# Attention values turned round: v as weights, the turned probabilities streamed, and a row's sums inverted once and spread by matmul

## What is computed

```python
x = x + _L0_conv_ref(_gn(x), ...)     # attention
x = x + _L1_conv_ref(_gn(x), ...)     # 3 x 3 convolution

# attention: 7 x 7 windows (N = 49 tokens), 8 heads of 16 channels
q = q * hd ** (-0.5)
attn = jnp.einsum('whnd,whmd->whnm', q, k)
attn = attn + jnp.transpose(rpb, (2, 0, 1))[None]      # and the mask of the shift
attn = jax.nn.softmax(attn, axis=-1)
x = jnp.einsum('whnm,whmd->whnd', attn, v).transpose(0, 2, 1, 3).reshape(B * nW, N, C)
x = x @ proj_weight.T + proj_bias
```

## Time and profile before

| | before |
|---|---|
| median of 3 runs (lowest to highest) | 3633.04 us (3629.91 to 3636.04) |
| profiled run: time, span | 3628.35 us, 3626.5 us |
| PE busy, PEld busy | 3415.0 us (94%), 2799.3 us (77%) |
| DVE, ACT, POOL busy | 3045.9 (84%), 2630.5 (73%), 2322.2 (64%) |
| matmul passes on PE | 57227 |
| values, transposes of the probabilities, scores: passes | 16384, 4096, 16384 |
| mean granted TensorE clock | 0.995 |

### The profile page before, as it was taken

How to read it: one execution, slowest core, us unless ns; L and a number is a source line. 1 busy time by engine, 2 the same in 40 slices (tenths; PEclk the granted TensorE clock), 3 DMA queues, 4 the chain that set the end, 5 groups by cost and what they waited for, 6 DMA issues and landing times.

```text
span 3626.5 us, 141183 instructions
## 1 busy us (share of the span) xinstructions
PE 3415.0 (94%) x57227; PEld 2799.3 (77%) x57227; DVE 3045.9 (84%) x7552; ACT 2630.5 (73%) x5857; POOL 2322.2 (64%) x3674
## 2 busy tenths in 40 slices
PE   2999999999999999999999999999999999999997
PEld 1778778778778778778777778777778778788785
DVE  5788888888888888888888888888888888888885
ACT  1777777777777777777777777777777777777772
POOL 4476666766666766666766666766667766657763
PEclk9999999999999999999999999999999999999998
DMA  2011101111101111101111111111111111111001
GB/s 57 20 30 33 33 25 30 36 33 36 33 25 30 36 33 36 33 23 33 35 34 35 28 28 33 33 35 36 28 28 33 33 36 33 30 25 33 18 18 29
DMA packets 213331, 113.75 MB, mean 31 GB/s; under 512 B 8784, under 2 KB 212688, under 8 KB 212688
## 3 DMA queue, kind: packets, MB, share of 16 engines
q1 hardware_dynamic: 212688, 104.72, 11.0%
HBM read 53.31 MB, written 51.38 MB: 29 GB/s over the span
## 4 chain that ended last, share of the span: by engine, by line
PE 51%; DVE 23%; POOL 12%; issue 11%; ACT 2%; SPq 0%; DVEq 0%; POOLq 0%; DMA 0%; ACTq 0%
PE conv_ps L994 14%; PE qkv_ps L875 10%; PE attn_ps L913 7%; PE probsT_ps L899 7%; PE scores_ps L888 5%; DVE s_sb L743 4%; POOL s_sb L404 3%; DVE plane_lo L755 3%; PE misc_ps L875 2%; DVE s_max L748 2%; DVE x_b L791 2%; PE misc_ps L961 2%; PE misc_ps L957 2%; PE misc_ps L951 2%; POOL x_n L444 1%
## 5 line engine op out<-in xcount | busy, mean ns | idle before, releaser
L404 POOL TENSOR_TENSOR s_sb<-s_sb,s_max 113x392 f32<-113x392 f32 x1024 | 1027.7, 1004 | 1127.6 <-DVE s_max L748 1123.2
L899 PE MATMUL probsT_ps<-ident,probs 113*128 113x113 f32 x4096 | 586.4, 265 | 72.6 <-ACT probsT L466 72.5
L460 ACT ACTIVATE probs<-s_sb 113x392 f32<-113x392 f32 x1024 | 551.6, 539 | 128.3 <-POOL s_sb L404 124.8
L432 POOL TENSOR_TENSOR plane<-x_n 128x224 f32<-128x224 f32 x896 | 601.3, 692 | 18.7
L913 PEld LDWEIGHTS attn_ps<-v,probsT 128*49 128x49 f32 x16384 | 465.4, 125 | 181.9 <-issue 160.3
L748 DVE TENSOR_REDUCE s_max<-s_sb 113x8 f32<-113x392 f32 x1024 | 574.6, 561 | 35.3
L527 ACT COPY v<-qkv_ps 64x256 f32<-64x256 f32 (+2 forms) x1280 | 393.6, 327 | 287.7 <-PE qkv_ps L875 281.6
L466 ACT COPY probsT<-probsT_ps 128x392 f32<-128x392 f32 x1024 | 489.5, 478 | 144.6 <-PE probsT_ps L899 140.4
L743 DVE TENSOR_TENSOR s_sb<-scores_ps,bias 113x392 f32<-113x392 f32 x1024 | 564.7, 551 | 8.1 <-PE scores_ps L888 8.1
L913 PE MATMUL attn_ps<-v,probsT 128*49 128x34 f32 x16384 | 566.5, 214 | 3.5 <-DVE o_sb L719 0.6
L899 PEld LDWEIGHTS probsT_ps<-ident,probs 113*128 113x128 f32 x4096 | 431.4, 141 | 129.3 <-ACT probs L460 86.0
(11 more groups left out here) (142 smaller groups left out, 6706.9 us busy)
## 6 DMA issues: line engine op xcount, KB each, us to landing
x_in<-in_x_dram SPq DMA_DIRECT2D x224, 224.0 KB, 2.8
out_dram<-x_out SPq DMA_DIRECT2D x224, 224.0 KB, 2.5
x_b<-in_L_conv_w_dram SPq DMA_DIRECT2D x1, 576.0 KB
x_b<-L_conv_pruning_mask_dram SPq DMA_DIRECT2D x1, 576.0 KB
x_n<-_conv_rel_pos_table_dram SPq DMA_DIRECT2D x14, 10.7 KB
x_n<-in_mask_dram SPq DMA_DIRECT2D x1, 196.0 KB
w_in<-n_L_conv_qkv_weight_dram SPq DMA_DIRECT2D x1, 192.0 KB
ident<-in_ident_dram SPq DMA_DIRECT2D x1, 64.0 KB
```

The source lines that it names most:

```text
L404: nc.gpsimd.tensor_tensor(s, s, top, ALU.subtract).then_inc(sub_ready, 1)
L432: last = nc.gpsimd.tensor_tensor(plane[:, t % 2, j], *sums[j])
L460: nc.scalar.activation(probs[0:QP, slot % 2, :, :, 0:N], s_sb[0:QP, slot % 4], ACT.Exp)\
L899: last = nc.tensor.transpose(probsT_ps[:, w * 128:w * 128 + QP], probs[0:QP, u % 2, w].rearrange("p e m -> p (e m)"), ident[0:QP, 0:QP])
```

## The change

The values are made once per row, at unit 2 of the next turn (`VALUES_AT = 6`), for all four pairs of heads. Now v is the weights (32 columns: a pair of heads) and the turned probabilities are streamed (49 columns); pair p goes to output partitions 32p to 32p + 31, so the result has channels on the partitions. The four turned units of a row are kept in six slots. The columns of ones in v go. Instead, a second group of matmuls in the same block has constant weights `head_ones` (32 columns, ones for one head in one column of its own for each window) and sums the exponentials over the windows of a row into 49 columns: partition 32p + 2w + e has head 2p + e of window w.

ACT copies the values to `values_sb`; DVE inverts the sums (128 x 49); at the end of unit 3 PE spreads the inverses over the channels (job "rec", 8 matmuls with constant weights `head_rows`, 128 columns, 49 streamed); DVE multiplies the values by them at the head of the next unit 0; ACT rounds to f16 in unit 0; DVE takes what is left at the head of unit 1; PE projects at the end of unit 1, as before, and now waits for that by name. The transposes of `o_sb` go. For room, `x_out` has two slots, and the set-up's weights lie in `plane`. POOL makes the two constants in the set-up.

```diff
+PT_SLOTS = 6
+VALUES_AT = 6
+OUT_SLOTS = 2
-LAG_T, LAG_PV = 2, 3
+LAG_T = 2
-        for first, kind in ((OT_AT, "ot"), (PROJ_AT, "proj")):
+        for first, kind in ((OT_AT, "rec"), (PROJ_AT, "proj")):
+def row_of(i, u, first):
+    r, rest = divmod(u - first, PAIRS)
+    turn, r = divmod(r, ROWS)
+    return (i + turn) * ROWS + r if rest == 0 and live(i, turn) else None
...
 # POOL, set-up
+            nc.gpsimd.memset(head_ones[:], 0.0).then_inc(head_consts, 1)
+            pool.wait_ge(head_consts, 1)
+            for e in range(2):
+                for a in range(2):
+                    diagonal = flat(head_ones)[ODD * e:ODD * e + ODD, a * HD + e::2 * HD + 2]
+                    nc.gpsimd.memset(diagonal, 1.0).then_inc(head_consts, 1)
+                    pool.wait_ge(head_consts, 2 + 2 * e + a)
+            rows = ident[:].rearrange("k (p x) -> k p x", x=2 * HD)
+            for w in range(NWIN):
+                last = nc.gpsimd.tensor_copy(
+                    head_rows[:, w, :].rearrange("k (p e d) -> k p e d", e=2, d=HD),
+                    rows[:, :, 2 * w:2 * w + 2].unsqueeze(3).to_broadcast((128, PAIRS, 2, HD)))
+            last.then_inc(head_consts, 1)
...
 # ACT
             def evacuate_probsT(i, g, slot):
                 act.wait_ge(probsT_ready, g + 1)
-                need(act, attn_ready, g - 1)
+                if g >= PT_SLOTS:
+                    act.wait_ge(attn_ready, (g - PT_SLOTS) // PAIRS + 1)
...
+                    row = row_of(i, u, VALUES_AT + 2)
+                    if row is not None:
+                        act.wait_ge(misc_free, rec_number(row) + 1)
+                        nc.scalar.copy(oT_hi[:].rearrange("p r (w c) -> p w r c", c=WIN),
+                                       o_sb[:].rearrange("p w (r c) -> p w r c", c=WIN)).then_inc(oT_hi_ready, 1)
                     misc(i, u, MID)
+                    row = row_of(i, u, VALUES_AT)
+                    if row is not None:
+                        act.wait_ge(attn_ready, row + 1)
+                        if row > 0:
+                            act.wait_ge(misc_free, rec_number(row - 1) + 1)
+                        nc.scalar.copy(values_sb[:], attn_ps[:, 0:RT].rearrange("p (w n) -> p w n", n=N))\
+                            .then_inc(values_copied, 1)
...
 # DVE
+                    row = row_of(i, u, VALUES_AT + 1)
+                    if row is not None:
+                        dve.wait_ge(attn_ready, row + 1)
+                        dve.wait_ge(values_copied, row + 1)
+                        vec.reciprocal(recip[:], attn_ps[:, RT:RT + N]).then_inc(recip_ready, 1)
+                    row = row_of(i, u, VALUES_AT + 3)
+                    if row is not None:
+                        dve.wait_ge(oT_hi_ready, row + 1)
+                        vec.tensor_tensor(oT_lo[:]..., o_sb[:]..., oT_hi[:]..., ALU.subtract).then_inc(oT_lo_ready, 1)
                     for kind, t in misc_at(i + turn, at):
+                        if kind == "rec":
+                            dve.wait_ge(misc_ready, misc_number(i + turn, kind, t) + 1)
+                            vec.tensor_tensor(o_sb[:], misc_ps[:, 0:RT]..., values_sb[:], ALU.mult).then_inc(misc_free, 1)
...
 # PE
-            def values(i, u):
+            def values(row):
+                pe.wait_ge(probsT_sb, (row + 1) * PAIRS)
+                pe.wait_ge(qkv_free, (row + 1) * 4)
+                need(pe, values_copied, row)
+                need(pe, recip_ready, row)
+                for w, pair in product(range(NWIN), range(PAIRS)):
+                    parts = slice(2 * HD * pair, 2 * HD * (pair + 1))
+                    mm(attn_ps[parts, w * N:(w + 1) * N], v[:, row % 2, w, pair, :],
+                       probsT[:, (row * PAIRS + pair) % PT_SLOTS, w, :], start=True, stop=True)
+                for w, pair in product(range(NWIN), range(PAIRS)):
+                    parts = slice(2 * HD * pair, 2 * HD * (pair + 1))
+                    last = mm(attn_ps[parts, RT:RT + N], head_ones[:, w, :],
+                              probsT[:, (row * PAIRS + pair) % PT_SLOTS, w, :],
+                              start=(w == 0), stop=(w == NWIN - 1))
...
+                if kind == "rec":
+                    pe.wait_ge(recip_ready, i * ROWS + (t + 1 if u >= OT_AT else t + 1 - ROWS))
+                    for w in range(NWIN):
+                        last = mm(misc_ps[:, w * N:(w + 1) * N], head_rows[:, w, :], recip[:], start=True, stop=True)
                 if kind == "proj":
+                    pe.wait_ge(oT_lo_ready, i * ROWS + (t + 1 if u >= PROJ_AT else t + 1 - ROWS))
...
+                    row = row_of(i, u, VALUES_AT)
+                    if row is not None:
+                        values(row)
                     if live(i, 0 if u // PAIRS < ROWS - 1 else 1):
                         qkv(i, u)
```

## The result

The median went from 3631.47 us (3629.73 to 3636.04) to 3872.39 us (3871.49 to 3874.91 in four runs): a ratio of 1.0662, 95% interval 1.0644 to 1.0681, so 241 us slower. The profiled run took 3872.84 us with a span of 3871.0. The forecast was 3835 in a range of 3735 to 3985.

The account below looks back on a forecast made before the run. The prediction took PE, busy 94% of the span, as what a change's cost is read on. It summed 3628.35 + 235 (PE's added work) - 32 (idle filled) = 3832 and said 3835 us, range 3735 to 3985.

Parts of the forecast that it names:

- The net on PE: PE work per row, added less removed: 1.62 + 1.78 - 2.09 - 0.39 = +0.92 us, +235 us over 256 rows.
- The new block: One PE block per row, 64 value and 64 sum passes with array switches, priced at 1.62 us.
- 43 ns a round: Four column tiles side by side in the block take one f32 stream of 49 columns; bounds 43 to 92 ns.
- What left: The old values blocks of a row's four units on PE, with their array-shape switches: 2.09 us a row.
- The spreading: PE's 8 f32 matmuls spreading the inverses, 16 passes paced by weight loads at 0.11 us: 1.78 us a row.
- the first rival: In the block, four column tiles run as two or share a port: 4230 us, partial losses between; chance 0.13.
- the case's own range: Main forecast's range from the idle's bounds and 0.15 us a row either way on switches: 3745 to 3920 us.
- The idle that fills up: Of PE's 3.6 us idle an image, longer rows fill 1 us: -32 us, bounds 0 and -115.
- DVE below 80%: Sign expected in the profile after: DVE's busy share of the span falls below 80%, from 84%.
- A new wait: Relay before the projection, or the wait for all four turned units, reaches PE: 3960 us if 1.6 later; chance 0.09.
- Weight loads that hide: Spreading passes run at their stream's 43 ns, costing 0.69 us a row: about 3550 us; chance 0.05.
- DVE or POOL as the bound: PE's 0.92 us falls into gaps and DVE's 0.47 a row counts: 3510 us or about nothing; chance 0.05.

Follow-up runs that it names:

- pair_outer: Changed kernel with the pair of heads as outer loop and the window inner, so 16 passes in a row go to one column tile: 4583.02 us.
- lo_on_pool: Changed kernel with the subtraction giving oT_lo moved from DVE in unit 1 to POOL in unit 0: 3956.20 us.
- no_sums: Changed kernel without the 64 sum passes of a row, inverses taken of a constant, output not the reference's: 3700.30 us.
- no_spread: Changed kernel with one f32 spreading matmul of 392 streamed columns instead of 8 with 49, output not the reference's: 3677.25 us.
- swap_alone: Changed kernel without the sums and most of the spreading, leaving the operand swap and its relay, output not the reference's: 3520.23 us.
- spread_tiles: Changed kernel with each window's 128 x 128 spreading matmul replaced by four 32 x 32 f32 ones on the array's diagonal: 3695.53 us.
- spread_f16: Changed kernel with spreading weights in f16 and the inverses as two f16 parts, adding two small DVE operations: 3731.78 us.
- split_sums: Changed kernel with the 64 sum passes moved from behind the values to behind the same unit's qkv passes: 3898.47 us.
- two_units_a_block: Kernel before, unswapped, with the values of two units in one block ahead of qkv in even units: 3626.40 us.
- f16_late: spread_f16 with DVE's inversion moved from the head of unit 3 to behind that unit's maximum: 3706.72 us.

## Why the prediction came out as it did

**What goes, what comes.** The net on PE was put at +0.92 us a row and full rows went from 13.06 to 13.96, +0.90. The new block was put at 1.62 and reads 1.66. 43 ns a round measured 45. What left, 2.09, can't be read after; from the row it is 1.66 + 1.37 - 0.90 = 2.13, with 1.37 for the spreading less the turn (1.91 - 0.54). The spreading was put at 1.78 and the turn at 0.39; both leave out some 0.14 us before the scores, so the difference (1.39 against 1.37) was right while each was small. +235 us stands: 256 x 0.90 = 230.

**The sums as written.** Three small ones don't come out. The point is 3628.35 + 235 - 32 = 3831, not 3832; the first rival's block is 3.14 - 1.62 = 1.52 us longer, not 1.55 (4220, not 4230); and from the idle's bounds and 0.15 us a row the case's own range is 3710 to 3902, not 3745 to 3920. The measured 3872 lies in both.

**Four tiles at once.** The choice of 43 ns out of 43 to 92 was right, and its reason half wrong: pair_outer shows that the order of the code decides.
By the Trainium skill, TensorEngine Tiling, Instruction Overhead, each matmul has about 60 cycles; passes at 11 ns (26 cycles at 2.4 GHz) are shorter than that, so the rule doesn't hold here for passes on different tiles. Nor does the 2.38 times for three column tiles, of the Trainium skill, TensorE: Matmul & The Clock Gate, Part 3, carry over: four gave 44/11.3, 3.9 times, with the 44 ns of a pass alone in pair_outer.

**The idle that fills up.** Taken at -32 us out of 0 to -115. PE's idle without the new gaps (64.1/32 = 2.0 us an image) fell from 3.6 us an image to 1.5, so 2.1 us an image, -67 in all. The waits view has 43 of them in the one wait that the prediction named: 72.5 us for the turned probabilities became 29.6. The rest is in two waits that it didn't name (the kernel before, 140 to 3560 us):

```profile
PE conv_ps L994 <- DVE plane_lo L755: 18.1, 29, 0.6
PE misc_ps L972 <- DVE gn_var L682: 18.0, 31, 1.6
```

In the kernel after (140 to 3800) these are 0.2 and 0.5, while waits for ACT's q and v grew from 2.5 to 18.8. So the step was right in kind and half in size, and its reason was not the one given: the prediction let only DVE's saved half microsecond help, at one wait; DVE saved nothing (below), and PE waited less at three places. That longer rows with the same norm leave DVE and POOL more slack is argued; no run changed the norm.

**What was missing.** The gaps, 87 of them, 64 us by the waits and some 80 from start to start, were in no step and no rival. 235 - 67 + 64 to 80 = 232 to 248, and the measured difference is 241. The point was 37 low because the gaps were absent (64 to 80) and the idle's relief small (35 more): two errors of opposite signs, the first the larger. That the point came so near is in part luck.

**DVE.** Its gain of 0.47 us a row was to come from three operations, 521 us becoming 1.57 x 256 = 402. The groups of the kernel after (busy us, mean ns, idle before), against the earlier trace rows:

```profile
L760 DVE TENSOR_TENSOR oT_lo<-o_sb,oT_hi 128x392 f16<-128x392 f32 x256 | 262.1, 1024 | 7.9 <-ACT oT_hi L544 3.1
L770 DVE TENSOR_TENSOR o_sb<-misc_ps,values_sb 128x392 f32<-128x392 f32 x256 | 144.9, 566 | 171.7 <-PE misc_ps L1001 168.9
L755 DVE RECIPROCAL recip<-attn_ps 128x49 f32<-128x49 f32 x256 | 119.8, 468 | 144.8 <-ACT values_sb L553 141.3
```

The reciprocal (455 said, 468 read) and the multiply (551, 566) are right. The subtraction was taken at the 565 ns that it took out of PSUM and takes 1024 out of SBUF. So the three sum to 526.8 us and DVE won nothing. In 223 of its 256 cases an operation of POOL over a whole tile overlaps it, and it takes 0.67 to 1.22 us; in the other 33, 31 of them beside the norm's one-column steps on POOL, it takes 0.56 to 0.58.
The Trainium skill, SBUF — State Buffer, section SBUF: two separate sides, says that a DVE operation with two SBUF inputs and a GpSimd operation that reads SBUF take turns at a shared port pair, the later one waiting; the 1024 ns against 565 agree with it, and the prediction should have applied it when the operand moved from PSUM to SBUF. The order shows in tok_lo, a subtraction of the same size out of SBUF (L874): in the 71 cases where POOL's operation begins inside it, it takes 0.56 to 0.61 us.
It cost nothing here because PE is full; "DVE below 80%" of the signs was barely met (3081.6/3871.0 = 79.6%), by the longer span and not by less work: DVE's busy time rose by 36 us.

**The rivals.** Fewer tiles at a time: not so (11 ns a pass), though pair_outer shows the way to it, 4583. A new wait: PE has none for the relay; lo_on_pool is what it would look like, 3956. That this is near the rival's 3960 is chance, since half of its loss is the clock's. Weight loads that hide: 110 ns apart as in the earlier trace rows; with f16 weights they are 25 apart. DVE or POOL as the bound: the chain has PE at 76%.

**What stays open.** What is taken off PE comes back only in part: 68% (no_sums), 72% (no_spread), 67% (swap_alone), 64% (spread_tiles), 39% (spread_f16). Idle at the norms and half-clock stretches add up to 94, 72, 182 and 180 us in no_sums, no_spread, swap_alone and spread_f16, where 80, 76, 171 and 221 are missing: they are the cause in the main, but how it splits isn't settled, and no run shows what decides which idle is followed by the low clock. That the gaps are starved instruction fetches rests on their timing beside the packets (87 of 87) and on what the length and the density of the block do (none in its place in no_sums and pair_outer, 44 of 87 left in split_sums); no run changed the fetch itself. Why the sums by themselves still stall in split_sums, and the values by themselves not in no_sums, is open.

## What to carry to other kernels

When a swap of weights and stream makes short passes cheap, price what the old layout gave for free: here the ones column of v became 64 passes and a per-partition scale became a matmul with 128-column f32 weights, and together they cost three times what the swap won. Put matmuls of different column tiles next to each other in the program, and keep weights that are only ones and zeros in f16, if what that asks of the other engines is paid for: here the f16 spreading took 1.41 us a row off PE and lost the most of it again, and the four f32 tiles, with nothing new on DVE, ended faster. Where PE is full, a microsecond taken from it gave back some 0.7 here, and 0.4 where DVE got work in exchange.

## What the runs showed of the hardware

- Overlap of column tiles depends on the order: 11 ns a pass with the tiles in turn, 37 with each tile's passes in a row (44 within a tile; a change of tile saves some three passes' worth).
- A dense stretch of 256 PE instructions in 1.4 us stalls now and then (53 times in 256 rows, up to 1.8 us) with no data to wait for, and its followers 34 times more. A stretch of 128 in 0.7 us did 33 times in split_sums, where another such stretch runs ahead of it, and never in no_sums. Each of the 87 ends 1.2 to 1.6 us after a 16 KB packet of the instruction queue.
- With 128 x 128 weights and 49 columns streamed, passes stand 110 ns apart in f32 and 25 in f16; on four 32 x 32 tiles in f32, 11.
- The granted clock went to 0.50 for 3.4 to 10 us after some long idles of PE and not after others. Of the idles of 1.2 us or more in the steady part, 3 of 30 were followed by it in the kernel before, 1 of 15 after, 14 of 28 in no_sums, 13 of 36 in no_spread, 30 of 59 in swap_alone, 24 of 48 in spread_f16, 28 of 61 in two_units_a_block and 2 of 21 in f16_late. So it is the kernels with less work on PE that have 13 to 32 such stretches, but f16_late is one of them and has 2, and lo_on_pool, not relieved, has 20: its projection waits.
- A DVE subtraction of 392 elements takes 0.56 to 0.58 us out of SBUF, alone or beside the norm's one-column steps on POOL, and 0.67 to 1.22 beside POOL's operations over whole tiles; with one operand in PSUM (the kernel before) it takes 0.55 to 0.58 either way. Where POOL's operation begins after it, it isn't slowed (tok_lo, 71 cases, 0.56 to 0.61).
